# Latent attention: scores made twice, operands loaded for four heads at a time, and a diagonal block put together on GpSimd

## What is computed

```python
q = x @ Wq; k = x @ Wk; v = x @ Wv                       # x normalised by layer
latent_kv = (k + v) @ W_down_kv                          # 64 wide
k_rec, v_rec = latent_kv @ W_up_k, latent_kv @ W_up_v
scores = clip(einsum(heads(q), heads(k_rec)) / 16, -1e4, 1e4)   # 16 heads of 16, S = 1024
scores = clip(scores * exp(-1e-4 * abs(i - j)), -1e4, 1e4)
out = softmax(scores) @ heads(v_rec)                     # then @ Wo, added to x
```

## Time and profile before

| | us |
|---|---|
| median of 3 runs | 1616.47 |
| profiled execution | 1615.76 |
| its span, first to last instruction | 1614.2 |
| TensorE busy | 1340.0 (83%) |
| VectorE busy | 919.8 (57%) |
| ScalarE busy | 930.1 (58%) |
| GpSimd busy | 190.5 (12%) |

### The profile page before, as it was taken

How to read it: one execution, slowest core, us unless ns; L and a number is a source line. 1 busy time by engine, 2 the same in 40 slices (tenths; PEclk the granted TensorE clock), 3 DMA queues, 4 the chain that set the end, 5 groups by cost and what they waited for, 6 DMA issues and landing times. The chain is left out here.

```text
span 1614.2 us, 36474 instructions
## 1 busy us (share of the span) xinstructions
PE 1340.0 (83%) x12288; PEld 960.2 (59%) x12291; DVE 919.8 (57%) x2059; ACT 930.1 (58%) x1793; POOL 190.5 (12%) x546
## 2 busy tenths in 40 slices
PE   5879999999999995898365699889874489999992
PEld 2347777777777774544223464364354279999992
DVE  5558888888888873532788844563354223323233
ACT  2469999999999991355375377624631033333330
POOL 0001111111111110111200000031120701111110
PEclk9879999999999997899756899988995589999996
DMA  3311010010101013200000100033006211111115
GB/s 115 131 51 31 22 27 24 24 26 23 29 20 29 20 38 110 80 1 4 16 1 0 31 1 1 1 120 129 1 4 212 102 34 36 37 36 38 36 33 166
DMA packets 60025, 74.30 MB, mean 46 GB/s; under 512 B 13006, under 2 KB 47728, under 8 KB 59952
## 3 DMA queue, kind: packets, MB, share of 16 engines
q1 hardware_dynamic: 53168, 56.76, 11.9%
q0 software_dynamic: 4672, 14.50, 2.7%
q10 hardware_dynamic: 2112, 2.10, 0.4%
HBM read 50.43 MB, written 22.88 MB: 45 GB/s over the span
## 5 line engine op out<-in xcount | busy, mean ns | idle before, releaser
L659 DVE CUSTOM_DVE_ANT_0 probs_sb<-banks,decay_sb 128x1024 f32<-128x1024 f32 x256 | 308.2, 1221 | 43.6 <-PE banks L578 22.5
L706 ACT ACTIVATE probs_sb<-probs_sb,shift_sb 128x1024 f32<-128x1024 f32 x256 | 294.8, 1151 | 18.1 <-POOL shift_sb L563 16.4
L588 PEld LDWEIGHTS banks<-ident_sb,probs_sb 128*128 128x128 f32 x2048 | 238.3, 141 | 55.1 <-issue 22.9
L588 PE MATMUL banks<-ident_sb,probs_sb 128*128 128x128 f32 x2048 | 267.8, 274 | 0.9 <-ACT probs_t_sb L521 0.8
L521 ACT ACTIVATE probs_t_sb<-banks 128x512 f32<-128x512 f32 x384 | 214.7, 597 | 4.1 <-PE banks L588 2.3
L578 PE MATMUL banks<-k_stack_sb,q_stack_sb 96*128 96x512 bf16 x512 | 156.9, 389 | 14.0 <-DMA k_stack_sb<-k_parts 10.7
L603 PE MATMUL banks<-probs_t_sb,v_head_sb 128*32 128x128 f32 x4096 | 151.2, 277 | 0.7 <-ACT probs_t_sb L521 0.7
L1846 PEld LDWEIGHTS banks<-slots_xt_sb,tile_w_sb 128*128 128x128 f32 x1248 | 146.5, 193 | 1.9
L1846 PE MATMUL banks<-slots_xt_sb,tile_w_sb 128*128 128x128 f32 x1248 | 146.6, 276 | 0.0
L1858 PE MATMUL banks<-experts_w_sb,xt_sb 128*128 x624 | 141.2, 379 | 1.3 <-issue 1.3
L1892 ACT ACTIVATE slots_xt_sb<-banks 128x256 f32<-128x256 f32 x39 | 14.9, 383 | 213.8 <-PE banks L1832 213.8
(11 more groups left out here) (289 smaller groups left out, 1910.0 us busy)
## 6 DMA issues: line engine op xcount, KB each, us to landing
experts_w_sb<-in_L_ffn_W SPq DMA_DIRECT2D x16, 1024.0 KB, 11.9
q_stack_sb<-q_parts SPq DMA_DIRECT2D x192, 32.0 KB, 1.7
k_stack_sb<-k_parts SPq DMA_DIRECT2D x192, 32.0 KB, 1.8
slots_x<-zeros_sb POOLq DMA_DIRECT2D x1, 5031.0 KB, 22.6
slots_x_sb<-slots_x SPq DMA_DIRECT2D x39, 129.0 KB, 2.1
xt_sb<-outputs_y SPq DMA_DIRECT2D x8, 512.0 KB, 5.5
q_parts<-parts_sb SPq DMA_DIRECT2D x8, 384.0 KB, 3.0
k_parts<-parts_sb SPq DMA_DIRECT2D x8, 384.0 KB, 4.2
```

Source lines behind the costliest of these rows:

```text
L588: last = pe.transpose(k.ps[:, 4 + half, j * P:(j + 1) * P], pr[:, s % 4, (half * TPG + j) * P:(half * TPG + j + 1) * P], k.ident[:, :])
L659: dve.tensor_tensor_reduce(out=pr[:, s % 4, :], in0=scores, in1=decay[:, off:off + S], scale=1.0, scalar=-3.0e38, op0=ALU.mult, op1=ALU.ma ...
L706: act.activation(pr[:, s % 4, :], pr[:, s % 4, :], ACT.Exp, bias=shift[:, s % 8:s % 8 + 1], accum_out=sums[:, (s // TPG) % 4, s % 4:s % 4 ...
```

## The change

**Projections.** exp(-c|i-j|) is a product of a factor of the query's and one of the key's position, with opposite signs on the two sides of the diagonal. So each piece is made in two versions (32 in place of 16): VectorE multiplies by the position factor (`apply_fade`), ScalarE makes the first part out of it, VectorE subtracts it, ScalarE makes the second, and **GpSimd** the third. The channels of q and k are reordered on the host so that the rows of four heads lie together. The two tables of 0.94 MB are loaded in this block (`later`), no longer ahead of it. From the 21st version on SP loads the first group's stacks.

**Attention.** 16 groups: 4 heads by 512 queries. A stack holds four heads; SP loads it in 6 pieces for the queries and, every second group, 6 for the keys (131 to 393 KB each for keys, half for queries), at the start of the group before the last. There are 96 rows and 3 more.

- `scores` makes a tile as before, but in two or three matmuls, one side of the diagonal from each version. VectorE (`highest`) takes its maxima; the products are thrown away. The table `inner` corrects the block on the diagonal.
- The maxima of 16 tiles are split in three bf16 parts on GpSimd, turned on TensorE, copied by ScalarE and stored by a DMA as rows 96 to 98 of the query stack; against them the key stack has rows of -1.
- A group has 8 steps, one for each tile of 128 keys. `key_scores` makes the scores again with keys on the partitions and 512 queries along the columns, maxima already subtracted, for 4 heads; ScalarE takes four exponentials of 512 columns. No turning is left. On odd steps the key tile crosses the diagonal: there `diagonal_scores` makes the block with the other version for all 4 heads, and GpSimd zeroes the wrong triangle of both halves and adds them (`select`), ahead of the step's value sums.
- `sum_values` sums values and, through a column of ones, the exponentials: four heads side by side, 512 columns. It stands two steps behind its exponentials in TensorE's order. Three banks (4 to 6) go round as a ring for all that ScalarE or VectorE reads except tiles and sums.
- Tiles run ahead: 22 before the first step, then two a step. `clear_slots` stays behind all of GpSimd's work.

```diff
+            def apply_fade(e):
+                n, version = divmod(e, 2)
+                dve.wait_ge(qk_ready, n + 1)
+                wait(dve, part3_done, e - 3)
+                side = version if is_query(e) else 1 - version
+                half = n // 4 % 2
+                dve.scalar_tensor_tensor(out=rest[:, e % 4, :], in0=k.ps[:, n % 4, :], scalar=scale if is_query(e) else 1.0,
+                                         in1=fade[:, side, half * G:(half + 1) * G],
+                                         op0=ALU.mult, op1=ALU.mult).then_inc(faded, 1)
+            def subtract_first(e):
+                dve.wait_ge(part1_done, e + 1)
+                dve.tensor_tensor(rest[:, e % 4, :], rest[:, e % 4, :], parts[:, e % SLOTS, 0, :],
+                                  ALU.subtract).then_inc(rest1_done, 1)
+                if bounds(e):
+                    own.did(dve.tensor_reduce(largest[:, e // 2:e // 2 + 1], parts[:, e % SLOTS, 0, :], AX, ALU.max,
+                                              apply_absolute_value=True))
+            dve.wait_ge(fade_arrived, 2 * 16)
...
+        @block.gpsimd
+        def _(pool):
+            for e in range(NV):
+                pool.wait_ge(part2_done, e + 1)
+                pool.wait_ge(rest1_done, e + 1)
+                pool.tensor_tensor(parts[:, e % SLOTS, 2, :], rest[:, e % 4, :], parts[:, e % SLOTS, 1, :],
+                                   ALU.subtract).then_inc(part3_done, 1)
...
+    version, r = divmod(piece, 3)
+    copies, row = 3 - r, HD * [0, 3, 5][r]
+    dst = slice(row, row + copies * HD)
+    if half == 0:
+        eng.dma_start(stacks.k[dst, n % 2, version, :, :].rearrange("p h n -> p (h n)"),
+                      stacks.k_scratch[version, 0:copies, rows, :].rearrange("c (p h) n -> c p (h n)", h=HEADS)).then_inc(stacks.arrived[g % 3], 16)
+    eng.dma_start(stacks.q[dst, g % 3, version, :, :].rearrange("p h n -> p (h n)"),
+                  stacks.q_scratch[version, r, half, rows, :].rearrange("(p h) n -> p (h n)", h=HEADS)
+                  .unsqueeze(0).to_broadcast([copies, HD, HEADS * G])).then_inc(stacks.arrived[g % 3], 16)
+def stacks_arrived(eng, stacks, g):
...
+        return 4 + place[item] % 3
+    def wait_for_bank(pe, item):
+        if place[item] >= 3:
+            pe.wait_ge(*ring[place[item] - 3])
     with ExitStack() as c, nc.Block() as block:
...
+            def scores(tile):
+                g, x = divmod(tile, TILES)
+                h, j = divmod(x, TPG)
+                if x == 0:
+                    stacks_arrived(pe, stacks, g)
+                wait(pe, peaked, tile - 1)
+                edge = (g % 2 * TPG + j + 1) * P
+                for version in range(2):
+                    for half in range(2):
+                        lo, hi = max(half * G, 0 if version == 0 else edge), min((half + 1) * G, edge if version == 0 else S)
+                        if lo < hi:
+                            last = pe.matmul(k.ps[:, 2 * (tile % 2) + half, lo - half * G:hi - half * G],
+                                             stacks.q[0:ROWS, g % 3, version, h, j * P:(j + 1) * P],
+                                             stacks.k[0:ROWS, g // 2 % 2, version, h, lo:hi], start=True, stop=True)
+                last.then_inc(scored, 1)
...
+            def key_scores(g, i, h):
+                item = (exp_done, unit_index(g, i, h) + 1)
+                if i == 0 and h == 0:
+                    pe.wait_ge(peaks_in, (g + 1) * 16)
+                wait_for_bank(pe, item)
+                edge = min(max(block_of(g, i) * P, 0), G)
+                if edge > 0:
+                    last = key_product(g, i, h, bank_of(item), 1, 0, edge, 0)
+                if edge < G:
+                    last = key_product(g, i, h, bank_of(item), 0, edge, G, edge)
+                last.then_inc(key_scored, 1)
...
+            def diagonal_scores(g, i):
+                item = (exp_done, unit_index(g, i, HEADS) + 1)
+                wait_for_bank(pe, item)
+                lo = block_of(g, i) * P
+                for h in range(HEADS):
+                    last = key_product(g, i, h, bank_of(item), 1, lo, lo + P, h * P)
+                last.then_inc(key_scored, 1)
+            def sum_values(s):
+                g, i = divmod(s, QT)
+                n, kt = g // 2, key_tile(g, i)
+                pe.wait_ge(exp_done, unit_index(g, i, HEADS if on_diagonal(i) else HEADS - 1) + 1)
+                if i == 0:
+                    pe.wait_ge(v_staged, n + 1)
+                    wait(pe, mix_copied, g)
+                if on_diagonal(i):
+                    pe.wait_ge(merged, s // 2 + 1)
+                for h in range(HEADS):
+                    last = pe.matmul(k.ps[VW * h:VW * (h + 1), PV_BANK, :], vh[:, n % 2, h, kt, :], probs_of(s)[:, h, :],
+                                     start=i == 0, stop=i == QT - 1, skip_group_check=True)
+                last.then_inc(summed, 1)
...
+            for tile in range(TILES + LEAD):
+                scores(tile)
+                if tile == TILES + 1:
+                    turn_peaks(0)
+            for g in range(GROUPS):
+                for i in range(QT):
+                    if g * QT + i >= 2:
+                        sum_values(g * QT + i - 2)
+                    for x in range(2):
+                        for h in range(2 * x, 2 * x + 2):
+                            key_scores(g, i, h)
+                        if x == 1 and i == TURN_STEP and g + 1 < GROUPS:
+                            turn_peaks(g + 1)
+                        if tile_at(g, i, x) < GROUPS * TILES:
+                            scores(tile_at(g, i, x))
+                    if on_diagonal(i):
+                        diagonal_scores(g, i)
+                    if i == 3 and g > 0:
+                        turn_mix(g - 1)
+            for s in range(GROUPS * QT - 2, GROUPS * QT):
+                sum_values(s)
+            turn_mix(GROUPS - 1)
...
+            def select(g, i):
+                s = g * QT + i
+                lo = block_of(g, i) * P
+                later = probs_of(s)[:, :, lo:lo + P]
+                pool.wait_ge(exp_done, unit_index(g, i, HEADS - 1) + 1)
+                pool.affine_select(later, later, [[0, HEADS], [1, P]], ALU.is_ge, 0.0, base=0,
+                                   channel_multiplier=-1).then_inc(selected, 1)
+                earlier = probs_d[:, s // 2 % 2, :, :]
+                pool.wait_ge(exp_done, unit_index(g, i, HEADS) + 1)
+                pool.affine_select(earlier, earlier, [[0, HEADS], [-1, P]], ALU.is_gt, 0.0, base=0,
+                                   channel_multiplier=1).then_inc(selected, 1)
+                pool.wait_ge(selected, 2 * (s // 2 + 1))
+                pool.tensor_tensor(later, later, earlier, ALU.add).then_inc(merged, 1)
+            own.wait()
+            stage_values(0)
+            split_peaks(0)
...
+                    if i == 3 and g % 2 == 0 and g + 2 < GROUPS:
+                        stage_values(g // 2 + 1)
+                    if i == TURN_STEP - 1 and g + 1 < GROUPS:
+                        split_peaks(g + 1)
             clear_slots(k, pool, zeros_set)
-
...
+                wait(dve, peaked, tile - 1)
                 dve.nop(nofuse=True)
-                dve.tensor_tensor_reduce(out=pr[:, s % 4, :], in0=scores, in1=decay[:, off:off + S],
+                dve.tensor_tensor_reduce(out=junk[:, tile % 2, :], in0=tile_scores(tile), in1=inner[:, window(tile)],
                                          scale=1.0, scalar=-3.0e38, op0=ALU.mult, op1=ALU.max,
-                                         accum_out=peak[:, s % 8:s % 8 + 1]).then_inc(peaked, 1)
-
-            def trailing(i, s, due):
...
+            def exponential(g, i, h):
+                u, s = unit_index(g, i, h), g * QT + i
+                act.wait_ge(key_scored, u + 1)
+                act.wait_ge(released, u + 1)
+                if h == 0:
+                    wait(act, summed, s - 2)
+                if h < HEADS:
+                    out = probs_of(s)[:, h, :]
+                else:
+                    wait(act, merged, s // 2 - 1)
+                    out = probs_d[:, s // 2 % 2, :, :].rearrange("p h n -> p (h n)")
+                act.activation(out, k.ps[:, bank_of((exp_done, u + 1)), :], ACT.Exp).then_inc(exp_done, 1)
```

585 lines of the change are left out of this document (328 added, 257 removed).

## The result

The changed kernel takes **1750.09 us**, the median of 4 runs (1749.05 to 1753.71), against 1616.40 (1615.93 to 1617.06) for the kernel before in the same session: ratio 1.0831, 95% interval 1.0812 to 1.0850, 134 us slower. The prediction was 1596, with a range of 1540 to 1690: wrong in sign, and the time lies outside the range.

A forecast was written before the change was run, and what follows sets the result against it. ScalarE and TensorE were nearly always busy before; afterwards TensorE's wait for GpSimd would set the pace. Projections to 90, main part from 116.5 to 578.5, tail to 602.1, plus 992.0 unchanged: span 1594.1, forecast 1596 us, range 1540 to 1690.

The forecast's parts named there:

- Transfers cost nothing in this sum: Stack loads in attention: 2.4 MB wanted within 17 us needs 140 GB/s, taken as available, so no time was added.
- Rival 5: Stack loads arrive late: at 100 GB/s seven groups stall, 28 us in all, 1624 us; chance 0.06 shared with rival 4.
- rival 4: TensorE's clock falls in the main part: at 1.2 GHz some +360 us; chance 0.06 shared with Rival 5.
- Projections: Block before attention: 32 versions at 1.65 us each, ending at 90 us, bounds 85 and 98.
- Rival 3: In the projections, VectorE's and GpSimd's subtractions exclude each other: 2.05 us a version, +13 us, 1609; chance 0.08.
- Lead: Start of attention: scores at 90.5, 22 tiles of maxima in 26 us, main part from 116.5; the maxima's trip hides.
- The added wait: Odd steps: value sums wait for GpSimd's two selections and addition, making a pair of steps 7.15 us, not 6.4.
- Y: Time of GpSimd's selection on 128x512 in odd steps: taken as 0.9 us, with 0.52 and 1.9 for the range.
- L: Odd steps: time from TensorE issuing the diagonal unit until GpSimd's addition releases it, 3.8 us; a pair is L + 3.35.
- rival 1: GpSimd's selection is quick, near 0.52 us: a pair is 6.4, TensorE bounds, 48 us less, 1548 us; chance 0.20.
- TensorE's prices: Main part: value sum 1.00 us, 512-column bf16 matmul 0.22; 25.6 us a group, 6.4 a pair of steps.
- The tail: End of attention: clearing DMA queued behind GpSimd's last addition, 0.6 + 22.6 + 0.4 us, from 578.5 to 602.1.

The follow-up runs named there:

- e1: The changed kernel with every stack load cut into transfers of 16 rows, so that the outermost dimension is 16: 1602.7 us, ratio 0.9945.
- e4: The changed kernel with the first group's stacks loaded at the start of attention, not between the projections' stores: 1757.2 us, one run.
- e10: Changed kernel with 16-row loads, early clearing DMA, rows of -1 set behind the identity; GpSimd subtracts only 16 of 512 columns of third parts: 1572.8 us.
- e3: The changed kernel without any stack loads from the fourth group on, so its output is not the reference's: 1616.9 us, one run.
- e7: Changed kernel with 16-row loads, rows of -1 and clearing DMA early (1589.3 us), plus the second selection done twice: 1612.3 us.
- e8: e1 with the clearing DMA issued in the middle of the main part: 1587.5 us, ratio 0.9840.

## Why the prediction was wrong, point by point

Its sum gave a span of 1594.1; 1749.3 was measured. The 155.2 us, in the order of time:

| stretch | predicted | measured | off |
|---|---|---|---|
| block starts | 90.0 | 130.9 | +40.9 |
| to the first scores | 0.5 | 17.3 | +16.8 |
| to the first exponential | 26 | 31.9 | +5.9 |
| main part without the six waits | 462 | 435.2 | -26.8 |
| the six waits | 0 | 118.6 | +118.6 |
| last addition to next block | 23.6 | 22.7 | -0.9 |
| the rest | 992.0 | 992.6 | +0.6 |

- **The step that failed is "Transfers cost nothing in this sum".** It asked for 140 GB/s and found them in rows 8 and in the clearing DMA, which writes to all partitions. Rows 8 are transfers with 16 rows outermost; the diff puts copies outermost. Both figures were true of other shapes. Rival 5 is the case that came: transfers late was right, its size was not, and it named no reason. It took 100 GB/s and 4 us a group in seven groups, 28 us; it was 2.4 MB in 37 us, 65 GB/s, six waits of 20, 118.6 us, and with a part of the 0.06 that it shared with rival 4 it was all but excluded. The bound from below was missing: nothing in the trace of before showed a load of this shape, and the range took in no price for that.
- **Projections, 90, with bounds 85 to 98**: 130.9. Three terms. The first group's loads in SP's queue made 20 to 22 us (e1, e4); the sum put them at nothing. Rival 3 was right in its mechanism, 10 us against its 13 (e10). The other 10 were in sight: at each of the three turns from one group of tokens to the next VectorE waits 4.1 us for TensorE's products, 12.4 of the 18.1 us of L395 above (the rest lies ahead of the first product), and 32 x 1.65 has no term for them. In the kernel before ScalarE waits 3.33, 2.43 and 1.53 us for L350 at these turns.
- **Lead**: no price at all for setting the rows of -1, 13.75 us and on the path. Rows 7 could have bounded it: 0.52 us for 512 elements a partition is 1.0 ns each, some 17 us for 16384 of them. That only three partitions are written takes nothing off. The rest, +5.9, is mostly the way of the maxima into the query stack, which was said to hide. (The text has it go through DRAM; `store_peaks` moves them from buffer to buffer in one DMA.) They are copied at 170.97, and the first key scores wait until 179.51. In e1 the time from the first scores to the first exponential is 4.2 us shorter, 27.7 against 31.9, so most of it was the same slow queue.
- **The added wait** was right in its form, and its size came out by the measured Y. The selection takes 0.634 us, between the ends 0.52 and 1.9, not the 0.9 taken; the addition 1.267, as predicted (1.28). With that the text's own sum gives L = 3.25 and a pair of 6.6 us, and a main part of 427; pairs of 6.28 and 6.77 stand above, and e3 with no load in the way took 421.6. So Y was nearer rival 1's 0.52 than the forecast's 0.9. The chance went to Y, whose whole range was worth 176 us by that text, while its real share was under 30. By e7 a microsecond in the chain costs 0.58 a pair (0.41 / 0.71), not 1.
- **TensorE's prices** held: a value sum spaced 1.00 (301.53 to 302.52), 0.22 a matmul of 512 columns, granted clock 1.00 in 310 to 335 where it isn't stalled (e1). Rival 4, the clock, did not come, but for the waits for stacks: after a stall it starts at 0.50 (342 to 346 in the kernel after).
- **The tail** held: 22.7 against 23.6, and e8 shows that the clearing DMA alone made 15 of it.

Had the loads had 16 rows outermost as in the kernel before, e1's 1602.7 would have been the answer, inside the range and 0.55% below the kernel before. That nearness to 1596 would have been luck: against the sum, e1's span has the block 20.4 us late, the first scores 17.2 and the first exponential 1.7 more behind it, and the main part 24.5 and the tail 2.1 shorter.

## What to carry to other kernels

When a change alters the shape of a transfer, a landing time from the old shape is no price for it: compare the outermost dimension on both sides, and read the DMA share beside the GB/s: here a low rate at a share of 0.14 was a matter of shape and not of bandwidth. A step moved onto an idle engine costs what it holds up elsewhere: GpSimd's long set was on the path at the start of a block, stopped VectorE in the layer norm, and of the three places tried showed no cost only beside VectorE instructions that read PSUM. The last thing queued behind a block's work, here a DMA of 22 us, is worth moving before anything is tuned (11 us in the kernel before).

## What the runs showed of the hardware that was not expected

- Loads with three or two copies outermost kept 2.2 of 16 DMA engines busy at 55 GB/s, in a stall with never more than four packets open (325 to 340); with 16 rows outermost all 16 were busy, at 131 GB/s and not at seven times the rate. What limits it there is open.
- A set by GpSimd costs by the elements of a partition, not by the partitions: 3x16384 bf16 in 13.75 us (0.84 ns an element), 128x2048 float32 in 1.80 (0.88).
- A VectorE instruction of 0.17 us stood 12.90 behind that set; one that reads PSUM and a table in SBUF took its 1.22 to 1.23 us beside it.
- A selection by position on GpSimd, 128x512 float32, takes 0.634 us, half of an addition of two operands (1.267).
- One DMA issue stood 9.69 us in SP's queue while earlier loads were open, and everything behind it on that queue with it.
